# Turning dt to both partition halves on TensorE in six chunks, with rows and u asked for in steps 7 to 13

## What is computed

```python
x_hwwh = jnp.stack([x_flat, x_t], 1)                            # two orders of the 1024 tokens
xs = jnp.concatenate([x_hwwh, jnp.flip(x_hwwh, -1)], 1)         # and both reversed
x_dbl = jnp.einsum('bkdl,kcd->bkcl', xs, x_proj_w)
dts, Bs, Cs = jnp.split(x_dbl, [R, R + N], axis=2)
dts = jnp.einsum('bkrl,kdr->bkdl', dts, dt_projs_w)
dts = jax.nn.softplus(dts + dt_projs_b[None, :, :, None])       # 192 channels x 1024 tokens
As = -jnp.exp(A_logs).reshape(K, DI, N)
...
dA = jnp.exp(d_t[..., None] * As)                               # 16 states a channel
h = h * dA + (d_t * u_t)[..., None] * B_t[:, :, None, :]
y = jnp.einsum('bkcn,bkn->bkc', h, C_t)
```

## Time and profile before

| | |
|---|---|
| timed runs, median of 3 | 1,577.3 us (1,574.91 to 1,587.61) |
| the profiled execution | 1,595.89 us |
| its span, first to last instruction | 1,594.1 us |
| TensorE matmul busy | 1,351.7 us (85% of the span) |
| VectorE busy | 1,229.5 us (77%) |
| GpSimd busy | 1,025.6 us (64%) |
| ScalarE busy | 1,018.5 us (64%) |
| first scan to last scan | 188.6 to 1,306.0 us |
| mean granted TensorE clock | 0.938 |

### The profile page before, as it was taken

One profiled execution on the slowest core, in us unless ns is written; L12 is line 12 of the kernel. 1 busy time (PEld: TensorE's weight loads), 2 busy tenths in 40 slices (PEclk: granted clock), 3 DMA queues, 4 the chain that ended last, 5 costly groups with the idle time before them and its releaser, 6 DMA issues. The chain is left out here.

```text
span 1594.1 us, 66411 instructions
## 1 busy us (share of the span) xinstructions
PE 1351.7 (85%) x30388; PEld 830.5 (52%) x30388; DVE 1229.5 (77%) x1029; ACT 1018.5 (64%) x1957; POOL 1025.6 (64%) x294
## 2 busy tenths in 40 slices
PE   6997688888987888998788899878889886969998
PEld 5734455554554555555555555545555543535554
DVE  4876198989899898989989997997989884644220
ACT  3448677777778778787877877776787551311222
POOL 0002089989899998999899998988899980000000
PEclk8998879999999999999999999998999997789999
DMA  9243524233333423333342332334243326100111
GB/s 324 97 156 145 170 56 112 76 93 82 81 87 89 109 79 93 79 90 81 89 113 78 91 99 70 85 85 109 66 101 80 97 82 221 67 0 35 40 40 45
DMA packets 73479, 151.13 MB, mean 95 GB/s; under 512 B 33238, under 2 KB 41942, under 8 KB 72816
## 3 DMA queue, kind: packets, MB, share of 16 engines
q1 hardware_dynamic: 73200, 146.88, 32.1%
HBM read 101.76 MB, written 32.51 MB: 84 GB/s over the span
## 5 line engine op out<-in xcount | busy, mean ns | idle before, releaser
L1219 POOL TENSOR_TENSOR s_h<-s_h,s_crow 128x2048 f32<-128x2048 f32 (+1 forms) x256 | 880.1, 3468 | 159.3 <-DVE s_h L1183 159.3
L1183 DVE TENSOR_TENSOR_SCAN s_h<-s_a,s_pb 128x1024 f32<-128x1024 f32 x384 | 862.4, 2275 | 131.7 <-PE s_pb L1018 96.3
L1018 PE MATMUL s_pb<-k_area,m_dtut 64*64 64x64 f32 x24576 | 479.2, 226 | 149.6 <-DVE s_h L1183 98.7
L1018 PEld LDWEIGHTS s_pb<-k_area,m_dtut 64*64 64x64 f32 x24576 | 435.4, 139 | 325.1 <-DVE s_h L1183 161.9
L1058 PE MATMUL s_py<-s_h,k_eye 64*64 64x512 f32 x3072 | 431.7, 614 | 14.6 <-issue 8.3
L298 ACT ACTIVATE k_area<-k_mask,m_bt 128x64 f32<-128x64 f32 x992 | 273.3, 337 | 0.0
L1109 ACT ACTIVATE s_a<-y_y,m_aneg 128x1024 f32<-128x1024 f32 x192 | 219.0, 1142 | 54.1 <-DVE s_h L1183 53.9
L1109 ACT ACTIVATE s_a<-m_dup,m_aneg 128x1024 f32<-128x1024 f32 x192 | 219.3, 1143 | 32.5 <-DVE s_h L1183 32.5
L204 POOL TENSOR_TENSOR k_area<-m_bt,k_mask 128x2048 f32<-128x2048 f32 x33 | 145.0, 4396 | 128.9 <-ACT m_bt L273 128.9
L1058 PEld LDWEIGHTS s_py<-s_h,k_eye 64*64 64x64 f32 x3072 | 93.2, 138 | 41.4 <-issue 35.6
L270 ACT COPY y_y<-m_pm 128x384 f32<-128x384 f32 x60 | 28.8, 479 | 79.0 <-PE m_pm L224 79.0
(11 more groups left out here) (190 smaller groups left out, 1234.3 us busy)
## 6 DMA issues: line engine op xcount, KB each, us to landing
s_crow<-scratch_xd SPq DMA_DIRECT2D x256, 256.0 KB, 4.1
k_area<-in_x_dram SPq DMA_DIRECT2D x4, 1536.0 KB, 7.9
scratch_xt<-y_y SPq DMA_DIRECT2D x4, 1536.0 KB, 8.6
y_y<-y_y SPq DMA_DIRECT2D x24, 256.0 KB, 4.3
m_dup<-m_dup SPq DMA_DIRECT2D x24, 256.0 KB, 4.2
out_dram<-t_out SPq DMA_DIRECT2D x32, 192.0 KB, 1.9
k_area<-scratch_xt SPq DMA_DIRECT2D x3, 1536.0 KB, 6.8
scratch_xd<-h_dbl SPq DMA_DIRECT2D x8, 512.0 KB, 2.6
```

Source lines behind the costliest of these rows:

```text
L1018: mm = pe.matmul(pb[par * HALF:(par + 1) * HALF, step % 2, r * BANK + blk:(r + 1) * BANK:BLK], dtut[here, u % 2, blk, g * HALF:(g + 1) * H ...
L1183: nc.vector.tensor_tensor_scan(h[:, step % (TRIPLES * CG), f], a[:, step % RING, f], pb[:, step % 2, f], 0.0, ALU.mult, ALU.add).then_inc( ...
L1219: nc.gpsimd.tensor_tensor(here, here, c.unsqueeze(1).broadcast_to([P, groups.stop - groups.start, L]), ALU.mult).then_inc(hc_ready, 1)
```

## The change

The two halves of `dup` are both written by TensorE and copied by ScalarE, in six chunks in steps 15 to 20 (one for each group and half of the tokens), and the doubling by DMA is gone. A chunk holds, for each of eight blocks, a matmul with the identity into partitions 64 to 127 and a transpose into partitions 0 to 63. `decay` waits for the chunks' copies. In the head, the two additional chunks stand at the end, after the last tile of z. SyncE asks for `rows` of the unit after the next in n = 4, for u of the next order in n = 4 of a unit with s = 0 and o = 0, and for u of the next image in n = 5 of one with s = 0 and o = 1; `rows` of unit 1 stay where they were.

```diff
-    return order + [("DUP", i) for i in range(4)]
+    return order + [("DUP", i) for i in range(2 * CG)]
...
-    return {"Z": (0, 1, 2, 3), "BT": (4,), "UT": (5, 7, 10, 13), "DUP": (16, 17, 18, 19)}[what][i]
+    return {"Z": (0, 1, 2, 3), "BT": (4,), "UT": (5, 7, 10, 13), "DUP": (15, 16, 17, 18, 19, 20)}[what][i]
...
-    def double(self, sp, u, groups):
-
-        for g in groups:
-            sp.wait_ge(self.chunk_taken, CHUNK[u, "DUP", 1 if g < 2 else 3] + 1)
-            have = slice(HALF, P) if g == 1 else slice(0, HALF)
-            lack = slice(0, HALF) if g == 1 else slice(HALF, P)
-            sp.dma_start(self.dup[u % 2][lack, g], self.dup[u % 2][have, g]).then_inc(self.dup_in[g], 16)
...
         if what == "DUP":
             pe.wait_ge(self.dt_ready, ROUNDS * (u + 1))
-            r, chans = i % 2, slice(0, P) if i < 2 else slice(P, DI)
+            g, r = i // 2, i % 2
             here = slice(r * HALF, (r + 1) * HALF)
             for blk in range(BLK):
-                mm = pe.transpose(pm[0:chans.stop - chans.start, blk::BLK], self.dt_of[here, blk, chans], eye[here, here])
+                group = self.dt_of[here, blk, g * HALF:(g + 1) * HALF]
+                pe.matmul(pm[HALF:P, blk::BLK], group, eye[here, here], start=True, stop=True)
+                mm = pe.transpose(pm[0:HALF, blk::BLK], group, eye[here, here])
...
         if what == "DUP":
-            cols = halves()[i % 2]
-            if i < 2:
-                nc.scalar.copy(self.dup[u % 2][HALF:P, 1, cols], pm[HALF:P])
-            dst, src = self.dup[u % 2][0:HALF, 0 if i < 2 else 2, cols], pm[0:HALF]
+            dst, src = self.dup[u % 2][:, i // 2, halves()[i % 2]], pm[:]
...
-            m.double(sp, 0, range(CG))
...
             in_proj_z(1, range(7, TT))
+            m.chunk(pe, 0, "DUP", 4)
+            m.chunk(pe, 0, "DUP", 5)
...
             silu_z(1, range(7, TT))
+            m.take_chunk(act, 0, "DUP", 4)
+            m.take_chunk(act, 0, "DUP", 5)
...
-                    if n == 0 and u + 1 < UNITS:
-                        sp.wait_ge(chunk_done, CHUNK[u, "BT", 0] + 1)
-                        load_rows(sp, d, keep, shared, u + 1)
-                        if s == 1 and o == 0:
-                            sp.wait_ge(chunk_done, CHUNK[u - 1, "UT", 3] + 1)
-                            load_u(sp, d, keep, shared, b, "turned")
-                        if s == 1 and o == 1:
-                            sp.wait_ge(y_taken, 2 * (taken(b, 0) + 1))
-                            load_u(sp, d, keep, shared, b + 1, "flat")
+                    for soon in [1] if u == 0 and n == 0 else [u + 2] if n == 4 and u + 2 < UNITS else []:
+                        sp.wait_ge(chunk_done, CHUNK[soon - 1, "BT", 0] + 1)
+                        load_rows(sp, d, keep, shared, soon)
+                    if n == 4 and s == 0 and o == 0:
+                        sp.wait_ge(chunk_done, CHUNK[u, "UT", 3] + 1)
+                        load_u(sp, d, keep, shared, b, "turned")
+                    if n == 5 and s == 0 and o == 1 and b + 1 < BATCH:
+                        sp.wait_ge(y_taken, 2 * (taken(b, 0) + 1))
+                        load_u(sp, d, keep, shared, b + 1, "flat")
...
-                    if n == 6 and u + 1 < UNITS:
-                        m.double(sp, u + 1, range(2))
-                    if n == 7 and u + 1 < UNITS:
-                        m.double(sp, u + 1, range(2, CG))
...
-                    act.wait_ge(dup_in[g], 16 * (u + 1))
+                    act.wait_ge(chunk_taken, CHUNK[u, "DUP", 2 * g + 1] + 1)
```

More of the change, by code:

```diff
@@ L195, in __init__ @@
         self.b_row = sem("b_row")
-        self.dup_in = [sem(f"dup_in{g}") for g in range(CG)]
     def build_d(self, eng, tt, u, piece):
@@ L929, in scan @@
         log_ready, floor_ready, dt_ready, dtu_ready = m.log_ready, m.floor_ready, m.dt_ready, m.dtu_ready
-        dup_in, d_even, d_odd = m.dup_in, m.d_even, m.d_odd
+        d_even, d_odd = m.d_even, m.d_odd
         crow_in = [sem(f"crow_in{i}") for i in range(CROWS)]
```

## The result

The changed kernel takes 1,967.9 us, the median of four runs (1,963.8 to 1,980.6), beside 1,582.5 for four of the kernel before: slower by a ratio of 1.243, with an interval of 1.237 to 1.249. The forecast was 1,842. The number is that of the rival in which the lower clock holds for half of these steps (1,965).

A forecast was written before the change was run, and what follows sets the result against it. VectorE's in-order scans and TensorE were taken to limit in turns; 228 (chunks) - 10 (traffic) + 14 (head) + 33 (clock) = 265 us gave 1,861 profiled, 1,842 against the timed median, range 1,745 to 1,925 (wider: 1,700 to 1,985).

The forecast's parts named there:

- the rival in which the lower clock holds for half of these steps: TensorE at 0.50 for half of the chunk steps: 1,965; for all, 2,120; chance 0.09 for half or more.
- The chunk of dt: TensorE's alternating matmul and transpose pairs: 0.43 us a pair, 3.4 us a chunk (2.9 to 4.1).
- The clock: TensorE's granted clock falls after its stand in step 15 of every unit: 33 us in all (0 to 40).
- one such chunk a unit: One dt chunk a unit at the lower clock, 5.4 us instead of 3.4, after TensorE stands about 2.9 us.
- The prediction's terms: Whole kernel: 228 us for chunks in steps 15 to 20, -10 traffic, +14 head, +33 clock, together 265.
- a stretch at 1.00 in which TensorE was busy for 4.96 of 10 us: Profile row of the kernel before, cited against the lower clock holding through all six chunks.
- The side-by-side case: Matmul and transpose of a chunk overlap in the two partition halves: 1.1 us a chunk, 1,577 us; chance 0.10.
- The head: Two more chunks for unit 0, each dearer, before the first decay: 14 us (11 to 18).
- Traffic: Without the doubling by DMA, fewer of TensorE's stops for issue: 10 us gained (0 to 22).
- The rival that the stops are not the transfers' doing: TensorE's stops for issue stay, so the 10 us gain is missing: 1,852, inside the forecast; no separate chance.
- Rows and u: Their requests by SyncE in steps 7 to 13 cost nothing, except a late row now and then.
- ScalarE's copies: Six copies a unit before and after, over twice the partitions, priced alike, at nothing.

The follow-up runs named there:

- e11: Changed kernel with sixteen added records of the next step's spread behind each matmul and transpose pair in units 1 to 15: 2,083.3 us, ratio 1.317.
- e1: Changed kernel with all eight matmuls of a dt chunk first, then all eight transposes, same 24 records: 1,663.0 us, ratio 1.051.
- e4: Changed kernel with the same instructions, four pairs of each chunk before the sum and four behind it: median 2,129.0 us (2,079.7 to 2,151.6).
- e2: Changed kernel with the lower half also written by a matmul with the identity instead of a transpose: 1,626.2 us, ratio 1.027.
- e6: Kernel before without the doubling by DMA from the third unit on, so part of the decays is left out of the result: 1,564.7 us, ratio 0.985.
- e3: Kernel before with only the requests for rows and u moved to steps 7 to 13: 1,580.4 us, ratio 0.997.

## Why the prediction was right about the sign and 126 us short

- **The chunk of dt: right.** A pair was put at 0.43 us and a chunk at 3.4; measured 0.43 and 3.38, at clock 1.00. The reading behind it, that every change from one kind to the other is paid, is shown by 16, 8 and 2 changes a chunk at 3.38, 2.35 and 1.58 us. The Trainium skill's TensorEngine Tiling (Array Packing), Key Properties, has TensorE drain at a change of tiling mode and gives no price; the trace agrees that a change is paid, at 0.129 us, although both kinds carry the same 64*64 label here.
- **The clock: the step that failed.** The prediction took "one such chunk a unit, +2.0 to 2.2 or 33 us", because TensorE stands in step 15 until dt is whole. That part came true in ten of the fifteen units, where TensorE stands 2.7 to 2.9 us and the first chunk takes 4.7 to 5.1 us. This is the unit behind the one shown above:

```profile
543.07 0.45 PE L237 MATMUL m_pm<-k_eye,y_y 64*64 64x64 f32 x2 [2.89 <-DVE y_y L1155]
...
548.17 1.98 PE L1007 MATMUL s_pb<-k_area,m_dtut 64*64 64x64 f32 x64
```

```profile
543.10:548.10 5.00, 5.00 (x24) 3.19 (x24) 3.67 (x2) 0.00 (x0) 5.00 (x2) 0.50 0.35 89
```

  In an eleventh unit the first chunk is as slow, behind a stop for issue. In the other four, the one shown above among them, TensorE has sums of an earlier y to do meanwhile (L1017), and the first chunk takes 3.4 to 3.9. What the prediction did not have is the fall behind the chunks, without any stand: the spread and sum take 3.46 instead of 1.84. From the scan of step 16 to that of step 21, over the fifteen units, the clock is at 0.50 for 55% of the time. These five steps take 34.7 us in the mean instead of 5 x 5.25 = 26.25, 8.5 more. With the first chunk (4.55 in the mean instead of 3.4) that is 9.6 a unit where 2.2 was taken, 7.4 more. Over the scan stage a unit grew by 23.9 us (last scan less first scan: 1,688.4 - 211.9 against 1,306.0 - 188.6, over 15 units). The prediction's terms make (228 + 33 - 10) / 15 = 16.7, so 7.2 are missing, about what the clock term lacks. 7.2 x 15 = 108 us, and with the 9 of the head below that is all but 3 of the 120 between 1,861 and 1,980.6.
- **The evidence that misled.** Against a lower clock the prediction set a stretch at 1.00 in which TensorE was busy for 4.96 of 10 us. That row was read for the wrong quantity: after the change the engine is busy for 3.30 of 3.30 us in a chunk and the clock still falls to 0.50 behind it. The Trainium skill's TensorE: Matmul & The Clock Gate, HAM oscillation, tells of falls where TensorE idles between bursts of matmuls; by that rule no more than the stand in step 15 would have counted, as forecast. The trace agrees for that stand, as it does for the 2.41 us of e11 and the 2.22 of the earlier trace rows, and disagrees for the falls behind chunks without any idle time. e1 (same records, few changes, 1.00 from the second chunk on) and e11 (same changes, more work between, 0.50 for 13% of the time) point to how little the array does in a chunk. No run separates this from the rival that it is the transposes in a chunk that count for little. By which measure the chip judges is open.
- **The rivals.** The lower clock "for half of the steps" gave 1,965, the measured time; with its end at 2,120 it had 0.09. Its amount was right, its picture only in part: a clock at 0.50 through whole steps is e4's, while the changed kernel is mostly at 0.50 in half of each step. The measured time lies above the forecast's own range (1,745 to 1,925); the wider one (1,700 to 1,985) holds it only because a part of this rival was taken into it. The side-by-side case is real for two matmuls (e2) and not for a matmul beside a transpose.
- **The head: mis-sized.** 14 us were forecast (11 to 18), 23.3 came. A window in its third dt chunk, which took 5.12 us, shows 0.50 here too:

```profile
180.00:184.00 4.00, 4.00 (x20) 2.51 (x19) 0.00 (x0) 0.00 (x0) 0.00 (x0) 0.50 0.00 0
```

  With the chunks grouped (e1) the first scan comes at 199.3, 10.7 late, and with two matmuls (e2) at 191.5.
- **Traffic: right in kind, too small.** 10 us were taken, with 22 as the end; without the doubling e6 gained 21. The prediction read the stops for issue as late instructions, "which no row proves". The trace of the kernel before shows it. Its list of DMA queues has one for instructions (packets, MB, share of 16 engines), and each packet on it has 16,384 bytes:

```profile
q8 instruction: 240, 3.93, 1.1%
```

  Each of the 47 stops in front of the spread ends 1.2 to 1.7 us after such a packet has landed; these stretches make up 11% of the scan stage. The Trainium skill, Runtime: NRT & Kernel Launch, Instruction fetch mechanics, calls the cost of crossing a block of instructions mostly hidden; the trace agrees for most of the 227 packets of that stage, and not for the 47 stops, which cost TensorE 43.3 us. The rival that the stops are not the transfers' doing falls for steps 16 to 22 (26.1 us, 4.2 without the doubling). But the doubling is not all that brings them: e2 has none, and with its 32 records a chunk it has 27.6 us of stops in these steps. How the doubling delays the packets is not shown either: one takes 1.14 us in the mean with it and 1.13 without. In the result the stops went from 43.3 to 14.8. But TensorE is now the engine that is late, and how much of this is a gain is not shown.
- **Rows and u, ScalarE's copies: right, at nothing.** e3 shows the first. A copy over 128 partitions takes 586 ns, over 64 it took 580.

## What to carry to other kernels

Count how often TensorE goes from transposes to matmuls and back, and put equal ones together: the order alone was worth 305 us here. Where an engine's instructions are to be made sparse (small tiles, many changes), price the work behind them at the lower clock too, and look at the granted clock by stretches as short as the pattern, since the busy share does not show it. A transfer for which nobody waits can still cost: leave it out once and look.

## What the runs showed of the hardware that was not expected

- The granted clock fell to 0.50 behind chunks in which TensorE was busy without a gap (3.30 of 3.30 us), and rose again behind the spread and sum, over and over through steps 15 to 20.
- One pattern of instructions can stay at either level: two pairs by two ran 20.2 us at 0.50 (7.28 a step) and then 16.6 us at 1.00 (4.20 a step), in the same unit.
- Added work kept the clock up: with sixteen records of the spread behind each pair a step of 7.14 us ran at 1.00, and from the scan of step 16 to that of step 21 the clock was at 0.50 for 13% of the time, where it was 55% without them.
- TensorE's stops for "issue" are late instructions: all 47 in front of the spread end 1.2 to 1.7 us after a packet of 16,384 bytes has landed on the instruction queue.
- Two 64x64 matmuls into the two halves of the partitions start 0.01 us apart, even at clock 0.50, while a matmul and a transpose into the same two halves start one after the other at 1.00: 0.26 from the start of a matmul to its transpose (457.55 to 457.81) and 0.17 back.
